# A macaron network on one core: how a routed FFN finds its experts' tokens, where the scattered sums go, and when they are added

## What is computed

```
x = x + 0.5 * ffn0(ln(x))      routed0
x = x + attn0(ln(x))           attention0
x = x + 0.5 * ffn0(ln(x))      routed1
x = x + 0.5 * ffn1(ln(x))      gated0
x = x + attn1(ln(x))           attention1
x = x + 0.5 * ffn1(ln(x))      gated1
```

```
scores = softmax(x @ gate_w.T)                 # [T, 16]
topk_w, topk_i = top_k(scores, 4)              # weights divided by their sum
# each expert's tokens in order of token, cut at CAP = 128; free slots hold token T
buf[e, rank] = tok ; wbuf[e, rank] = weight
xg = xpad[buf]                                 # [16, 128, 256]
mid  = silu(xg @ w_gate) * (xg @ w_up)         # 176 wide
eout = (mid @ w_down) * wbuf
y = zeros(T + 1, h).at[buf].add(eout)[:T]
return y + silu(x @ sw_gate) * (x @ sw_up) @ sw_down     # 352 wide
```

## Time and profile before

| what | value |
|---|---|
| median of 3 runs | 2144.9 us (2144.11 to 2145.5) |
| the profiled execution | 2145.69 us, its span 2143.8 us |
| mean granted clock of TensorE | 0.992 of full speed |
| PE busy | 2026.5 us, 95% |
| DVE / ACT / POOL busy | 69% / 62% / 43% |
| bytes moved by DMA | 67.28 MB, 31 GB/s over the span |

### The profile page before, as it was taken

One profiled execution on the slowest core, in us unless ns is written; L12 is line 12 of the kernel. 1 busy time (PEld: TensorE's weight loads), 2 busy tenths in 40 slices (PEclk: granted clock), 3 DMA queues, 4 the chain that ended last, 5 costly groups with the idle time before them and its releaser, 6 DMA issues. The chain is left out here.

```text
span 2143.8 us, 41216 instructions
## 1 busy us (share of the span) xinstructions
PE 2026.5 (95%) x14170; PEld 1809.7 (84%) x14170; DVE 1477.7 (69%) x3613; ACT 1331.4 (62%) x3393; POOL 931.7 (43%) x904
## 2 busy tenths in 40 slices
PE   5897978989989999999999999999999999999899
PEld 3665865658879999999999999999999999998778
DVE  6645767635477777777787787777878778777643
ACT  4223643225367777777786787777778768776652
POOL 0342001445454553645546355364454545536242
PEclk9999989999999999999999999999999999999999
DMA  6353032552000000000000000000000000000010
GB/s 207 98 120 57 2 103 86 142 108 63 1 16 6 4 13 6 4 6 9 9 6 9 6 4 14 6 4 6 9 9 6 9 6 9 9 6 1 1 45 30
DMA packets 50989, 67.28 MB, mean 31 GB/s; under 512 B 10081, under 2 KB 36961, under 8 KB 50657
## 3 DMA queue, kind: packets, MB, share of 16 engines
q1 hardware_dynamic: 40416, 51.80, 7.8%
q0 software_dynamic: 10368, 12.85, 3.6%
HBM read 49.15 MB, written 15.48 MB: 30 GB/s over the span
## 5 line engine op out<-in xcount | busy, mean ns | idle before, releaser
L1167 ACT ACTIVATE phase_p<-phase_scores,phase_bias 128x512 f32<-128x512 f32 (+3 forms) x680 | 417.5, 628 | 109.8 <-DVE phase_bias L1155 108.2
L1212 DVE TENSOR_TENSOR phase_pt_lo<-phase_ring,phase_pt_hi 128x512 fp32r<-128x512 f32 (+3 forms) x680 | 390.8, 603 | 92.4 <-ACT phase_pt_hi L1207 88.7
L1207 ACT ACTIVATE phase_pt_hi<-phase_ring 128x512 fp32r<-128x512 f32 (+3 forms) x680 | 342.9, 535 | 115.0 <-PE phase_ring L1192 111.9
L1192 PE MATMUL phase_ring<-sb_ident,phase_p 128*128 128x128 f32 x2312 | 340.8, 274 | 8.2 <-ACT phase_p L1167 5.0
L132 PE MATMUL phase_y<-phase_pt_hi,phase_v_hi 128*128 128x256 f32 (+1 forms) x1152 | 342.9, 298 | 4.8 <-DVE phase_y_lo L2212 4.4
L133 PE MATMUL phase_y<-phase_pt_lo,phase_v_hi 128*128 128x256 f32 (+1 forms) x1152 | 324.0, 281 | 0.0
L134 PE MATMUL phase_y<-phase_pt_hi,phase_v_lo 128*128 128x256 f32 (+1 forms) x1152 | 323.7, 281 | 0.0
L1192 PEld LDWEIGHTS phase_ring<-sb_ident,phase_p 128*128 128x128 f32 x2312 | 270.8, 140 | 45.6 <-ACT phase_p L1167 13.1
L1148 DVE TENSOR_REDUCE phase_peaks<-phase_scores 128x1 f32<-128x512 f32 x408 | 272.6, 682 | 47.5 <-PE phase_scores L1135 44.9
L2235 POOL TENSOR_TENSOR phase_straight<-phase_rot,late_rope 64x512 f32<-64x512 f32 x128 | 164.0, 1281 | 273.9 <-ACT phase_rot L2107 273.8
L2252 POOL TENSOR_TENSOR sb_x<-sb_x,phase_part 128x512 f32<-128x512 f32 x128 | 165.8, 1296 | 254.5 <-ACT phase_part L2142 248.1
(11 more groups left out here) (280 smaller groups left out, 5017.9 us busy)
## 6 DMA issues: line engine op xcount, KB each, us to landing
phase_e_up<-expert_up SPq DMA_DIRECT2D x32, 352.0 KB, 3.7
phase_e_dn<-expert_down SPq DMA_DIRECT2D x32, 256.0 KB, 4.1
y_rows<-phase_zero SPq DMA_DIRECT2D x8, 512.0 KB, 9.5
xn_rows<-phase_ln_xn SPq DMA_DIRECT2D x8, 512.0 KB, 6.8
sb_x<-y_rows POOLq DMA_DIRECT2D x8, 512.0 KB, 10.7
late_raw_qk<-qk SPq DMA_DIRECT2D x16, 256.0 KB, 2.7
sb_x<-x SPq DMA_DIRECT2D x4, 512.0 KB, 6.2
phase_raw_up<-up SPq DMA_DIRECT2D x8, 256.0 KB, 4.6
```

What stands on the lines that cost most here:

```text
L1167: act.activation(self.p[:, at:at + width], self.scores[:, at:at + width], ACT.Exp, bias=self.bias[:, t % 2:t % 2 + 1], accum_out=self.sums ...
L1192: done = pe.transpose(bank[:, j * P:(j + 1) * P], self.p[:, (4 * place + j) * P:(4 * place + j + 1) * P], self.core.ident[:])
L1207: act.activation(hi, value, ACT.Copy).then_inc(*self.t_hi.one)
L1212: dve.tensor_tensor(lo, value, as_f32(hi), ALU.subtract).then_inc(*self.t_lo.one)
```

## The change

- **Finding slots.** All 16 experts are searched at once. A token's slot in its expert is split into its low 4 bits (together with a large number for experts it didn't choose) and its high 3. DVE makes one-hot rows of both: `hot_row` and `hot_tile` from the high part (8 operations each, times the row number within a tile, and times a tile number), `hot_low` from the low part (16 operations), 256 elements each. PE sums 16 products of `hot_row` with `hot_low` and 16 of `hot_tile` with `hot_low` in one bank; the result is masked, one more product (`pick`) spreads it, and a reduction leaves all row numbers. Three constants (`minor`, `major`, `same`) are made for it from the identity, in routed0 between two parts of the norm. The searches among the experts, ACT's copies, the turning and the warm-up matmuls go.
- **Banks and buffers.** Early pieces of the shared FFN alternate between two pairs of banks; sums get up to three; `down` alternates between two, so `h n` waits for ACT's copy of h n - 1 only. Six fetches are under way for four, out has four buffers for two.
- **Two y.** Even experts scatter into `y_rows[0]`, odd ones into `y_rows[1]`; a scatter waits for the one two before. Both are zeroed by SP.
- **Order.** Seven projections and four sums of the shared FFN (`BEHIND` = 11) stand behind the last expert, six blocks among the experts.
- **Adding y.** Eight accumulating DMAs (two y, four chunks) in the order `GROWN`; POOL issues five at the end of the routed stage and three in the next one. Statistics wait for both halves of a chunk. Warm-up matmuls at the start of attention 0 go from 55 to 22, in gated 0 from 46 to 20. Attention 0's norm becomes `ChunkNorm` with groups (0), (1, 2), (3), whose powers run on POOL. Gated 0's SP no longer waits for POOL's memset before it loads weights.

```diff
-        self.y_rows = nc.dram_tensor("y_rows", (T + CAP, H), F32).ap()
+        self.y_rows = [nc.dram_tensor(f"y_rows{b}", (T + CAP, H), F32).ap() for b in range(2)]
...
+    SLOTS, FETCHED = 4, 6
+    AMONG, BEHIND = 6, 11
...
+        fill(2)
+        order.append(shared[0].pop(0))
+        order += [("rank",), ("mark_rows",)]
+        fill(2)
+        order.append(("mark_low", 0))
         fill(1)
-        order += [("mark", 0), ("mark", 1)]
+        order.append(("mark_low", 1))
         fill(1)
-        order += [("find", 0), ("weights",), ("mark", 2), ("mark", 3)]
+        order += [("mark_tiles", 0), ("mark_tiles", 1)]
         fill(2)
-        order += [("found", 0), ("fetch", 0), ("fetch", 1), ("find", 1)]
...
+        order += [("find", 0), ("find", 1), ("weights",)]
+        fill(1)
+        order.append(("mask",))
+        fill(1)
+        order += [("pick",), *(("fetch", n) for n in range(self.FETCHED))]
+        fill(len(shared) - self.AMONG - self.BEHIND - 1)
...
+        order += [("x", 0), ("x", 1)]
         fill(1)
         order.append(("feed", 0))
...
+        spread, given = (len(shared) - self.BEHIND) / NE, 0.5
...
-                    pe.wait_ge(*self.weighed[tag, n - 1])
+                    pe.wait_ge(*self.h_copied[tag, n - 1])
...
+                for a in range(P // NE):
+                    dve.tensor_scalar(self.hot_row[:, :, a, :], self.high_b[:], float(NE * a), self.row_id[:], ALU.is_equal, ALU.mult)
+            elif what == "mark_low":
+                for b in range(NE // 2 * key[0], NE // 2 * (key[0] + 1)):
+                    done = dve.tensor_scalar(self.hot_low[:, b, :], self.low_b[:], float(b), None, ALU.is_equal)
...
+                if n >= 2:
+                    pool.wait_ge(*self.placed[n % 2][tag, n - 2])
...
+        for half, c in GROWN[:5]:
+            if half == 0:
+                pool.wait_ge(*self.added[tag, c, 1])
+            pool.wait_ge(*self.placed[half][tag, NE - 2 + half])
+            pool_grow(core, pool, self.then, half, c)
...
+GROWN = ((0, 0), (0, 1), (1, 0), (1, 1), (0, 2), (1, 2), (0, 3), (1, 3))
+
+def pool_grow(core, pool, tag, half, c):
+    y_in, where = core.loads(f"y_in{c}"), slice(4 * c, 4 * c + 4)
+    if half:
+        pool.wait_ge(*y_in[tag, 0])
+    pool.dma_start(core.x[:, where, :], core.y_rows[half][0:T, :].rearrange("(t p) h -> p t h", p=P)[:, where, :],
+                   accum_op=ALU.add).then_inc(*y_in.one)
...
-    IDLE = {("flip", 0, 0): 55, ("state", 0): 6, ("score", 0, 0, 0): 9, ("score", 0, 1, 0): 5}
+    IDLE = {("flip", 0, 0): 22, ("state", 0): 6, ("score", 0, 0, 0): 9, ("score", 0, 1, 0): 5}
...
-            self.core.keep_warm(pe, bank, 46)
+            self.core.keep_warm(pe, bank, 20)
```

More of the change, by code:

```diff
@@ L153, in __init__ @@
         self.x_in = [core.loads(f"x_in{c}") for c in range(NCH)]
-        self.y_in = [core.loads(f"y_in{c}") for c in range(NCH)]
         if first:
@@ new lines, in pe @@
+                    done = pe.matmul(self.find_ps.rearrange("p (b e) -> p b e", e=NE), hot[:, t].rearrange("p a e -> p (a e)"), self.hot_low[:, :, at],
+                                     start=which == 0 and t == 0, stop=which == 1 and t == NT - 1)
+                if which:
+                    done.then_inc(*self.summed.one)
+            elif what == "pick":
+                pe.wait_ge(*self.mask_done[tag])
+                pe.matmul(self.pick_ps, self.same[:].rearrange("p a j -> p (a j)"), self.masked[:].rearrange("p b e -> p (b e)"),
+                          start=True, stop=True).then_inc(*self.pick_done.one)
@@ L904, in dve @@
         core, tag = self.core, self.tag
+        if not self.start:
+            self.dve_constants(dve)
         dve.wait_ge(*self.gate_hi[tag])
@@ L1501, in __init__ @@
         late = {c: 4 for c in range(NCH)}
[L1502 to L1503 removed]
+        self.norm = ChunkNorm(core, sb, tag, [c for c in range(NCH) if c not in ahead], add_y=add_y, by_act={**late, 0: 2}, quick=(0,))
         self.norms = [self.norm]
```

365 lines of the change are left out of this document (171 added, 194 removed).

## The result

| | median | runs | ratio to before, 95% interval |
|---|---|---|---|
| before | 2144.94 us | 4, 2144.11 to 2145.5 | |
| changed | 2088.79 us | 4, 2085.64 to 2090.81 | 0.9737, 0.972 to 0.9754 |
| changed, measured again | 2090.26 us | 4, 2089.64 to 2090.42 | 0.9744, 0.9728 to 0.976 |

56 us less. The forecast was 2089.4, 0.6 us from the median. But two of its terms were wrong by 12 and 9 us in opposite directions, so that the number came this close is luck. The profiled execution took 2085.64 us, 4.7 less than the 2090.3 that the sum gave for it.

What follows compares the result with a forecast made beforehand. Bound taken as PE's work plus waits in two routed stages and the empty stretches behind them. Stages -23.0 and -22.4, boundaries -7.65 and -4.85, given back +2.5: -55.4 us, 2090.3 profiled, 2089.4 median, range 2072 to 2111.

Steps and rivals of the forecast that it cites:

- PE's work in a stage: In each routed stage, PE's work priced start to start falls from 115.1 to 98.7 us.
- Marks: On DVE in each routed stage, 32 marks of 256 elements take 8.5 us, between 4 and 10.6.
- a second operation: On DVE, 0.33 us for each of 16 marks with two operations, 0.2 for each of 16 that only compare.
- Marks with stride: Rival: 16 marks writing runs of 16 cost 1247 ns each, +14.6 us a stage, 2118 us; chance 0.04.
- late weights: Among the experts, PE waits 3 us per stage for expert weights, bounds 0 and 6.
- Small places: In each routed stage, PE waits 0.8 us at small places and the tail.
- what I do not see: In each routed stage, an allowance of 1.7 us for unseen waits of PE.
- waits stay: Rival: the 19.9 us of waits remain, 118.6 us a stage, sum -40.6, 2104 us; chance 0.16.
- DMA bounds the experts: Rival: with a 152 GB/s ceiling the experts take 71 us, 2126 us; decides below 220 GB/s; chance 0.06.
- 6.7 instead of 14.35: Boundary into attention 0: 5.44 us from norm statistics to transposes, 1.06 of switching and 0.2, so -7.65 us.
- y is late: Rival: the first chunk lands as late behind the stage as before, boundaries give nothing, 2102 us; chance 0.11.
- Given back: Attention 0's second norm on POOL, later chunks 2 and 3, gated 0's weights beside additions: 2.5 us, between 0 and 8.

Runs made afterwards that it cites:

- matmuls put back: Changed kernel with six more matmuls of 256 columns, result unread, ahead of each transpose of hidden rows but the first, 90 a stage: 2105.43 us, ratio 0.9819.
- without searches: Kernel before the change with two of its eight searches, experts 4 to 15 taking the rows of experts 0 to 3: 2116.03 us, ratio 0.9865.
- one down bank: Changed kernel with the transpose of an expert's hidden rows waiting for DVE's weighing of the expert before: 2102.58 us, ratio 0.9798.
- one place at a time: Changed kernel with each scatter waiting for the one before it, as if there were one y: 2143.77 us, ratio 0.9991.
- the runs with three additions: Changed kernel with three of eight additions of y issued in the routed stage, five in the next, in three orders: 2092.96, 2086.64 and 2089.75 us.

## Why the prediction was right, and where it was not

**PE's work in a stage: right, 97.6 for 98.7.** An expert takes 2.49 us for 2.63, and the 32 search matmuls 3.8 (twice 1.92) for 3.9. The 97.6 is busy time, the 98.7 a sum of prices from start to start, so they agree only within the few us by which these differ. The run with matmuls put back shows this work on the path one for one; without searches the stages fell by more than the matmuls' 13.3.

**Marks: 6.4 us for 8.5, inside 4 to 10.6.** The step that took one price for "a second operation" failed: the row marks (tensor_scalar, two operations) took 0.20 us start to start, the tile marks (scalar_tensor_tensor) 0.34, the comparing ones 0.14, near the lower bound of 0.13. The rule of the Trainium skill (VectorE: DVE Perf Modes, The perf-mode tier table) that bf16 tensor_scalar runs at the fourfold rate, which the trace of before could not bear out, fits the 0.14 of the comparing marks; the row marks, a tensor_scalar too, took 0.20, and the table has no row for the tile marks' operation. It named the comparing marks 1 to 2 us cheaper, and they were by 1.0 (16 x 0.064). Marks with stride (2118) did not come: what the stores in runs of 16 cost the row marks is at most the 0.06 us by which they exceed the comparing marks, and how much of that is the second operation was not tested.

**Timing of the front: right.** PE waits 1.4 us for the second search as forecast, and 0.4 for the first where 2.3 was forecast; rows are known at 62.5 for 63.2, and the first fetch is issued at 63.4; first feed 70.05 for 69.7. The first feed, a dozen steps along DVE and PE by hand, came out 0.4 us late on the clock. But the forecast counted from the start of the kernel before, and the changed stage begins 1.3 us later: from the first projection the first feed comes after 33.7 us for 34.6, 1.0 early, with errors on both sides.

**Waits: 7.5 us for 12.5.** The terms that failed are the 3 us for late weights, which were 0, and the 2.3 for the first search, which was 0.4. "Small places" and "what I do not see" had 2.5 together and came to 2.5: 1.0 more at the bank and the copy of x, 0.9 behind the rounding of the shared layer, 0.5 at the last expert. Neither allowance had a row behind it, and one of the two was right. These 5 us of waits and 1.1 of work are the 6 us by which each stage was better. The rival "waits stay" fell, and so did "DMA bounds the experts": 270 GB/s went through where I asked for 220 to hold. The run with one down bank puts 12 to 14 us on the second bank, the one with one place at a time 54 on the two y, each with the rest of the change in place.

**POOL just keeps up: right.** Its last scatter is issued 4.3 us behind PE's last down product (125.05 and 120.71).

**The boundary: wrong.** The step that failed is "6.7 instead of 14.35", in its part "behind 1.06 of switching". That chunk 0 is there when PE ends (landed at 140.7, PE's end 141.5), and that the norm then takes 5.4 us to the transposes, was right: in the runs with three additions the boundary was 6.4 and 6.5. But I took the switch between stages from a kernel whose POOL had nothing under way there. With five additions issued, the block is left only when the last has landed: 6.4 and 5.0 us of standing for 1.06 and 2.28, and then 22 warm-ups at a granted 0.68 (7.03 us for 4.91), which outlast the norm. Against the runs with three additions the standing costs 5.3 and 3.9 us and the slow warm-ups some 1.5 each. In gated 0 two more terms failed, towards the other side: 9.5 was forecast and 6.5 is what it takes once the drain is out of the way, since POOL came 1.0 us behind PE for the 2.7 and the 1.6 for MODIFY_POOL_CONFIG was 0 (the forecast had named that as possible). The rival "y is late" was nearest in its numbers (boundaries that give almost nothing), though its reason, a late chunk 0, is not the one.

**Given back: 0.3 for 2.5**, since all of chunks 0 and 1 and half of 2 are in before the next stage starts. That is the other side of the same coin: the three runs that left three additions in the stage won 12 us at the boundaries and gave 11 to 17 back, against the changed kernel's first profile.

So 2089.4 came out of -12, +9 and -2 us of error, and from a profiled execution that was 3 us faster than the median: the closeness is luck. The mechanism of the stages is shown by the runs, the boundary's was missing from the forecast and is shown by the drains. That fewer than five additions are the better cut was found only afterwards.

## What to carry to other kernels

In every run here a block that all engines leave together waited for the accumulating DMAs that its POOL had issued, read or not: an early issue across such a border is only free if it lands by about the time the other engines end (the drain ends 1.5 us behind the landing, and PE needs 1.06 us to leave in any case). Count what a change leaves under way at the border, and cut where both ends meet (here four additions, 4.5 to 6 us better than five; three were 3.6 us better than five where the later ones kept out of POOL's way, and no better where they did not). Allowances without a row behind them belong in the range rather than in the likeliest case: of the two here one was 3 us a stage too much.

## What the runs showed that I had not expected

- POOL's drain at the end of a block lasted 2.7 us in the kernel before and 7.5 to 10.3 with additions under way, and ended 1.5 to 1.6 us after the last landing wherever that can be read (142.3 and 140.8 with three additions, 147.6 and 146.0 with five).
- Indirect scatters with addition, one waiting for the other, stand 4.5 us apart on quiet DMA engines and up to 5.9 beside weight loads. Two targets let them stand 3.2 apart on average.
- A DMA share of 0.99 at 270 GB/s did not hold up PE: in that stretch it was busy 23.0 of 23.0 us. POOL did wait there for a scatter to land.
- Warm-up matmuls put into PE's idle stretch brought the next ones to full clock in attention 0 (4.91 us for 7.03), but the kernel was 3.6 us slower, with slow clock later. Slow clock at the first feed made a stage 1.4 us longer.
